# Two attention stages of a two-layer kernel: layer 0 in steps of all four heads, layer 1 with on-chip copies at its start and 0/1 matmuls at its end

## The reference

```python
# layer 0: 16 heads of 64, 4 key/value heads, 2 batches, causal, S = 1024
scores = einsum('bhqd,bhkd->bhqk', q, k) * scale + causal
out = einsum('bhqk,bhkd->bhqd', softmax(scores), v)
return out.reshape(B, S, 1024) @ Wo.T
# layer 1: 16 heads of 8, 4 key/value heads, rope and rmsnorm on q and k, causal
scores = einsum('bthd,bshd->bhts', q, k) / sqrt(8)
out = einsum('bhts,bshd->bthd', softmax(where(causal, scores, -inf)), v)
```

## Time and profile before

| | us |
|---|---|
| median of 3 executions (1544.16 to 1556.04) | 1551.67 |
| the profiled execution | 1549.17 |
| its span, first to last instruction | 1547.5 |
| PE busy (share of the span) | 1316.2 (85%) |
| DVE busy | 1002.8 (65%) |
| ACT busy | 678.9 (44%) |
| POOL busy | 157.7 (10%) |

### The profile page before, as it was taken

One profiled execution on the slowest core, in us unless ns is written; L12 is line 12 of the kernel. 1 busy time (PEld: TensorE's weight loads), 2 busy tenths in 40 slices (PEclk: granted clock), 3 DMA queues, 4 the chain that ended last, 5 costly groups with the idle time before them and its releaser, 6 DMA issues. The chain is left out here.

```text
span 1547.5 us, 19708 instructions
## 1 busy us (share of the span) xinstructions
PE 1316.2 (85%) x6224; PEld 806.3 (52%) x6224; DVE 1002.8 (65%) x1782; ACT 678.9 (44%) x1254; POOL 157.7 (10%) x357
## 2 busy tenths in 40 slices
PE   4789999999999999748999987415898988489997
PEld 3345555555555555435888865313343443156886
DVE  4646566564747472157999985746777875057998
ACT  2133434343333433233666655421466666225664
POOL 0001111111111111100000000211011111010000
PEclk9689999999999999966999997855899999568999
DMA  3110202021111201004777720043122221102220
GB/s 98 28 32 5 57 5 60 11 54 34 30 37 27 50 14 32 15 21 92 157 148 146 160 60 1 1 138 80 27 49 60 50 47 29 53 21 77 76 102 28
DMA packets 42400, 85.59 MB, mean 55 GB/s; under 512 B 13392, under 2 KB 31480, under 8 KB 37368
## 3 DMA queue, kind: packets, MB, share of 16 engines
q1 hardware_dynamic: 42336, 84.78, 23.1%
HBM read 67.38 MB, written 8.45 MB: 49 GB/s over the span
## 5 line engine op out<-in xcount | busy, mean ns | idle before, releaser
L652 ACT ACTIVATE shared<-ps 128x1024 f32<-128x1024 f32 (+7 forms) x256 | 165.8, 650 | 359.8 <-PE ps L501 359.2
L516 PE MATMUL ps<-shared,Vg 128*65 128x512 f32 (+3 forms) x768 | 291.0, 487 | 11.3 <-POOL shared L683 8.5
L1227 PE MATMUL ps<-qA 128*128 128x512 f32 x960 | 254.3, 402 | 10.1 <-POOL qA L1337 10.1
L567 DVE TENSOR_REDUCE mraw<-ps 128x1 f32<-128x512 f32 (+3 forms) x304 | 195.9, 659 | 90.0 <-PE ps L468 62.1
L969 DVE TENSOR_REDUCE mraw<-ps 128x2 f32<-128x1024 f32 (+3 forms) x160 | 173.9, 1114 | 77.5 <-PE ps L889 59.5
L1227 PEld LDWEIGHTS ps<-qA 128*128 128x128 f32 x960 | 183.1, 194 | 60.6 <-POOL qA L1337 11.8
L1013 ACT ACTIVATE shared<-ps 128x512 f32<-128x512 f32 (+2 forms) x320 | 154.4, 564 | 127.8 <-PE ps L905 127.5
L499 PE MATMUL ps<-qA,kH 128*128 128x512 f32 (+3 forms) x384 | 168.2, 446 | 2.7 <-DMA qB<-mT 2.7
L462 PE MATMUL ps<-kH,qA 128*128 128x512 f32 (+3 forms) x384 | 163.5, 466 | 6.0 <-DVE qA L560 2.8
L516 PEld LDWEIGHTS ps<-shared,Vg 128*65 128x65 f32 x768 | 98.4, 138 | 118.7 <-issue 83.7
L1239 PE MATMUL ps<-qA,kH 128*128 128x512 f32 x480 | 136.1, 392 | 4.1 <-DVE qA L1353 4.0
(11 more groups left out here) (229 smaller groups left out, 1561.4 us busy)
## 6 DMA issues: line engine op xcount, KB each, us to landing
shared<-comb SPq DMA_DIRECT2D x92, 256.0 KB, 4.3
qB<-qA SPq DMA_DIRECT2D x8, 1024.0 KB, 7.1
rB<-a0rec_dram SPq DMA_DIRECT2D x8, 1024.0 KB, 7.4
shared<-comb SPq DMA_DIRECT2D x7, 1024.0 KB, 4.4
q_split<-qA SPq DMA_DIRECT2D x8, 512.0 KB
qA<-q_split SPq DMA_DIRECT2D x16, 256.0 KB, 4.4
rB<-a1rec_dram SPq DMA_DIRECT2D x32, 128.0 KB, 2.7
e0wUp<-in_w SPq DMA_DIRECT2D x48, 64.0 KB, 4.6
```

Source lines behind the costliest of these rows:

```text
L516: ins = nc.tensor.matmul(O[0:65, lo:hi], k.Vg[par][:, kt, :], k.PT[:, slot % PTR, lo:hi], start=(kt == 0), stop=(kt == 4 * ch + 3))
L567: ins = nc.vector.tensor_reduce(out, bank[:, 0:n_h * width].rearrange("p (h w) -> p h w", w=width), AX, ALU.max)
L652: nc.scalar.activation(k.PT[:, slot % PTR, kt * P:S], score_banks(slot)[:, kt * P:S], ACT.Exp, scale=scale).then_inc(p_full, 1)
L1227: ins = nc.tensor.matmul(bank[0:M, :], w[par][:, at:at + M], h[:, cols], start=(r == 0), stop=(r == 2))
```

## The change

**Layer 0's attention** takes the form that layer 1's already has: 12 units (qc, kt) per group with all four heads, written out without a loop. Scores go to three banks of 512 columns. The values of a unit are 12 matmuls with 32 stationary columns: v is cut into two halves of 32 columns, two heads with two halves each fill the four column quarters (bank 5 for heads 0 and 1, bank 6 for 2 and 3), and four further matmuls with ones give the sums of the four heads, 32 times each, in bank 7. `Vg` and its copies are gone. Values come two steps behind the scores (LAG), P has three buffers (RING). Jobs are laid behind the score matmuls of a step only. O and sums are copied out twice per group, by ACT (one bank) and DVE (two). Group 0 starts scores of its first query half when that half is prepared, the second half's jobs are laid into steps 0 to 3; the last turn of a group ("turn" of its second half) runs in the first step of the group itself. For the last half of the last group, DVE takes the reciprocal of the sums in PSUM, two matmuls with a 0/1 matrix (`sel64`) bring them to the heads' rows, and DVE multiplies.

**Layer 1.** q and k of groups 0 and 1 are copied from SBUF to SBUF: 32 DMAs on SP and 32 on ACT's own queue, of 8 rows x 1024 columns each. For the other groups q is stored once rather than twice, in the next stage, by 12 DMAs that ACT issues ahead of its first exp; the load reads it twice. POOL clears group 2's buffers, which overlap `qh`, when these stores have landed. The last group's outputs go through two pairs of 0/1 matmuls (`pick`), a reciprocal of 512 columns and a product, straight into `oT`.

```diff
+    UNITS = [(0, kt) for kt in range(4)] + [(1, kt) for kt in range(TPB)]
+    NU = len(UNITS)
+    STEPS = NU * G
+    RING = 3
+    LAG = 2
+    SCORE_BANKS = 3
+    U = 1 + REP // 2
+
...
+        size = max(1, 512 // (512 - unit_lo(n)) // 2 * 2) if 512 - unit_lo(n) <= 256 else 1
+        return [tuple(range(h, h + size)) for h in range(0, REP, size)]
...
+    def woven(g):
+
+        some = [("max", g, 0, j) for j in range(len(MAXES[0]))]
+        more = [("max", g, 1, j) for j in range(len(MAXES[1]))]
+        out = [("proj", g, 0, u) for u in range(U)] + [("proj", g, 1, 0)]
+        out += some[0:3] + [("proj", g, 1, 1)] + some[3:6] + [("proj", g, 1, 2)] + some[6:]
+        return out + more[0:3] + [("turn", g, 0, 0)] + more[3:]
+
...
+    plan = {-1: jobs_of(0, 0)}
+    spread_over(jobs_of(0, 1), 0, 4)
+    spread_over(woven(1), 4, NU)
+    for g in range(2, G):
+        spread_over([("turn", g - 1, 1, 0)] + woven(g), NU * (g - 1), NU * g)
+    plan.setdefault(NU * (G - 1), []).insert(0, ("turn", G - 1, 1, 0))
+    for g in range(G):
+        plan.setdefault(NU * g + 10, []).append(("fin", g, 0, 0))
+        plan.setdefault(NU * (g + 1) + 6, []).append(("fin", g, 1, 0))
...
+        size = -(-len(fills) // len(heads))
+        return [(hs, fills[size * i:size * (i + 1)]) for i, hs in enumerate(heads)]
...
-        O = k.ps[:, 6 * 512:8 * 512]
...
+        O = [k.bank(5), k.bank(6)]
+        SUMS = k.bank(7)
...
+                def values(n):
...
+                        pe.wait_ge(o_act, 2 * g + qc)
+                        pe.wait_ge(o_dve, 2 * g + qc)
+                    lo = unit_lo(n)
+                    first, last = kt == 0, closes(n)
+                    for p in range(2):
+                        for i in range(2):
+                            for half in range(2):
+                                at = 2 * i + half
+                                v = k.V[:, b * TPB + kt, kv * hd + half * CT:kv * hd + (half + 1) * CT]
+                                nc.tensor.matmul(O[p][CT * at:CT * (at + 1), lo:512], v,
+                                                 probs(n)[:, 2 * p + i, lo:512], start=first, stop=last,
+                                                 skip_group_check=True)
+                    for h in range(REP):
+                        ins = nc.tensor.matmul(SUMS[CT * h:CT * (h + 1), lo:512], k.ones[:, 0:CT],
+                                               probs(n)[:, h, lo:512], start=first, stop=last, skip_group_check=True)
+                    ins.then_inc(pv_done, 1)
+
+                for idx in due[-1]:
+                    job(idx)
+                for n in range(STEPS + LAG):
+                    for at, (hs, fills) in enumerate(parts(n)):
+                        if hs:
+                            scores(n, first_score[n] + at, hs)
+                        for idx in fills:
+                            job(idx)
+                    if n >= LAG:
+                        values(n - LAG)
+                pe.wait_ge(o_dve, 2 * G)
+                for p in range(2):
+                    nc.tensor.matmul(score_bank(p), k.sel64[:, p, :], k.S64[:, :], start=True,
+                                     stop=True).then_inc(spread_full, 1)
+                job(index["fin", G - 1, 1, 0])
+
+            @block.vector
+            def _(dve):
...
+                def copy_out(n):
...
+                    nc.vector.tensor_copy(k.S64[:, :], SUMS)
+                    nc.vector.tensor_copy(k.oU64[:, 1, cols], O[1]).then_inc(o_dve, 1)
...
+                for n in range(STEPS + LAG):
+                    if n > LAG and closes(n - LAG - 1):
+                        copy_out(n - LAG - 1)
+                    at = n % NU
+                    if at in (3, 5) and n >= NU:
+                        (recips if at == 3 else normalise)(n // NU - 1, 1)
+                    if at in (7, 9):
+                        (recips if at == 7 else normalise)(n // NU, 0)
+                    for idx in due.get(n, []):
+                        take(idx)
+                cols = slice(512, 1024)
+                dve.wait_ge(pv_done, STEPS)
+                nc.vector.reciprocal(k.S64[:, :], SUMS).then_inc(o_dve, 1)
+                for p in range(2):
+                    dve.wait_ge(spread_full, p + 1)
+                    if p == 0:
+                        dve.wait_ge(o_act, 2 * G)
+                        dve.wait_ge(on_done, 2 * G - 2)
+                    ins = nc.vector.tensor_tensor(k.oN64[:, p, cols], k.oU64[:, p, cols], score_bank(p), ALU.mult)
...
+                nc.scalar.copy(k.oU64[:, 0, 512:1024], O[0])
+                nc.scalar.copy(k.oU64[:, 1, 512:1024], O[1]).then_inc(o_act, 1)
...
+                def pick(qc):
+
+                    pe.wait_ge(o_copied, 2 * (G - 1) + qc + 1)
+                    pe.wait_ge(x_free, NJ * G)
+                    for what in range(2):
+                        ins = nc.tensor.matmul(k.bank(3 + 2 * qc + what)[LAST, :], k.sel8[:, what, :],
+                                               oU[(G - 1) % 2][:, qc * 512:(qc + 1) * 512], start=True, stop=True)
+                    ins.then_inc(x_full, 1)
...
+                    if n == STEPS - 5:
+                        pick(0)
+                pick(1)
...
+                    nc.vector.reciprocal(k.rB[LAST, cols], k.bank(3 + 2 * qc)[LAST, :]).then_inc(rec_done, 1)
+                    dve.wait_ge(rec_done, G + qc)
+                    nc.vector.tensor_tensor(oT[LAST, S + qc * 512:S + (qc + 1) * 512], k.rB[LAST, cols],
+                                            k.bank(4 + 2 * qc)[LAST, :], ALU.mult)
...
+                for b in range(B):
+                    act.wait_ge(in_ld[b], landed(b))
+                for b in range(B):
+                    for part in range(2):
+                        cols = slice(part * T + b * S, part * T + (b + 1) * S)
+                        act.dma_start(q_dram[:, part * hd:(part + 1) * hd, b * S:(b + 1) * S],
+                                      qh[:, cols].bitcast(F32)).then_inc(stored, 16)
+                        for copy in range(2):
+                            at = (2 * part + copy) * hd
+                            act.dma_start(k_dram[:, at:at + hd, b * S:(b + 1) * S],
+                                          kh[:, cols].bitcast(F32)).then_inc(stored, 16)
...
+                pool.wait_ge(stored, 16 * STORES)
...
-                load(0)
-                load(1)
-                sp.wait_ge(cleared, 1)
-                load(2)
...
+                sp.wait_ge(stored, 16 * STORES)
+                load(2)
...
-                gather_sums(G - 1)
-                spread(G - 1)
-                store(G - 1)
-                sp.wait_ge(o_st, 16 * REP * G)
-                sp.dma_start(oT[:, S:T], o_dram[:, :, S:T].rearrange("h d q -> (h d) q")).then_inc(oT_ld, 16)
+                sp.dma_start(oT[0:LAST.start, S:T], o_dram[0:NH - REP, :, S:T].rearrange("h d q -> (h d) q"))\
+                    .then_inc(oT_ld, 16)
...
+                act.wait_ge(padded, 2)
+                for b in range(B):
+                    act.wait_ge(low, 2 * CPB * (b + 1))
+                    for part in range(2):
+                        src = kh[0:hd, part * T + b * S:part * T + (b + 1) * S].bitcast(F32)
+                        for copy in range(2):
+                            for i in range(2):
+                                at = 64 * i + (2 * part + copy) * hd
+                                act.dma_start(kZero[b][at:at + hd, :].bitcast(F32), src).then_inc(k.a1_in[b], 16)
+                                act.dma_start(kOne[b][at:at + hd, :].bitcast(F32), src).then_inc(k.a1_in[b], 16)
...
+                    for i in range(2):
+                        for j in range(2):
+                            head = (i + 2 * j) * hd
+                            for part in range(2):
+                                src = qh[head:head + hd, part * T + b * S:part * T + (b + 1) * S].bitcast(F32)
+                                for copy in range(2):
+                                    at = 64 * i + (2 * copy + part) * hd
+                                    sp.dma_start(Q[b][at:at + hd, j, :].bitcast(F32), src).then_inc(k.a1_in[b], 16)
```

731 lines of the change are left out of this document (371 added, 360 removed).

## The result

The changed kernel takes 1536.7 us in the median against 1547.1 for the kernel before, each run 20 times: a ratio of 0.9934, with a 95% interval of 0.9913 to 0.9956. That is 10 us of the 47 forecast. The profiled execution took 1542.7 us (span 1540.9), 6.6 us of span less than that of before.

The account below looks back on a forecast made before the run. PE was taken to set the pace of layer 0's groups at 72.6 us each. The terms -6 -4 -5 -13 -10 -9 sum to -47 us against the profiled 1549.2: 1502 us, range 1472 to 1542.

Parts of the forecast that it names:

- Layer 0, values: Layer 0's value matmuls: three sets of column quarters replace four heads' blocks, -4.5 us a group (-3.0 to -6.3).
- the rival of the halves: Value matmuls: two halves sharing one head's P run one after the other, 15.4 us a group more, 1625; chance 0.05.
- Layer 0, waits: Layer 0's jobs, now only between score matmuls, make PE wait: +3.5 us a group, bounds 0 and +9.5.
- The new waits: Layer 0: 5 us from units with many jobs plus 2 from DVE's copies and products: 7 us a group.
- The hand walk: Layer 0 unit with six maxima, followed: PE waits about 1.0 us, in some five of twelve units.
- The waits of before: Layer 0 in the kernel before: 3.5 us of waits a group, taken from 8.4 us beyond pure column time.
- DVE's order sets the pace: Rival, layer 0: DVE's fixed places hold all jobs, +9.5 us a group instead of +3.5, 1544; chance 0.20.
- Layer 0, head: Layer 0's start: first scores at 62 us, group 1 at 158 against 162, -4 us (-20 to +12).
- Last group and layer 0's tail: End of layer 0: last group without jobs -5 us; tail from values to y without DMAs -13 us.
- Layer 1, head: Before layer 1's attention: copies at 0.55 us each, stores delaying some 2 us, -10 us (0 to -18).
- Layer 1, tail: After layer 1's attention: matmuls, reciprocal and product replace three DMA round trips, 9 us, a gain of -9 (-7 to -11).
- the marks that were to show it: Trace signs, both layers: unit values 2.8 to 3.0 us, period 70 to 73, layer 1's first matmul 17 to 20, others.

Follow-up runs that it names:

- run 20: Not a label, only words of "each run 20 times": changed kernel and kernel before, 20 executions each, medians 1536.7 and 1547.1 us, ratio 0.9934.
- layer 1 alone: The change in layer 1 only, with layer 0 as in the kernel before; measured 0.9929 (0.9896 to 0.9962) of the kernel before.

## Why the prediction was wrong

- **Layer 0, values: direction right, size low.** Forecast -4.5 us a group (-3.0 to -6.3), measured -6.0. The quarters of one head's halves go side by side, so the rival of the halves is out. (The eight records of a block in the earlier trace rows do not start together but in two sets of four, 0.45 us apart; four at a time is all that the argument needs.)
- **Layer 0, waits: this step failed.** Forecast +3.5 us a group, bounds 0 and +9.5; a period of 74.2 with 6.0 us less of values makes it +7.6. The +3.5 were 7 us of new waits less 3.5 us of waits that the kernel before was to have had.
  - *The new waits.* The hand walk took a unit of six maxima and let it stand for all. It left out what the upper bound had named, a projection whose bank is held through ACT's rounding and DVE's subtraction. Two of them stand between maxima in the fifth unit; moving them took 1.8 us a group, and with it the fall of the clock, which the sum had put at full throughout, 1.0. The other 4.8 of the 7.6 are the turnaround of two banks, for which the sum had 7 - 3.5: a third bank took 3.5 us, short reductions 5.1.
  - *The waits of before.* By the rows of waits PE's jobs waited 0.5 us a group for DVE before (the values 1.1 for POOL), not 3.5. With moved projections and short reductions, where little is left to wait for, a group takes 66.3 us, only 0.3 less than 72.6 - 6.0; so the 72.6 can hardly have had 3.5 us of such waits. That is worked out and not shown: no run has the kernel before with short reductions.

  The rival "DVE's order sets the pace" (+9.5) was nearer than the forecast, though the runs name two banks and not the order: a copy taken off DVE gave 0.2, the place of the maxima 0.5, a third bank with DVE's order as it was 3.9. The Trainium skill (TensorEngine Tiling (Array Packing), PSUM Bottleneck) warns that tiling speeds up TensorE and not the emptying of PSUM; the runs agree, with 3.5 to 6.0 us a group, though the banks that held PE were those of the jobs, which are not tiled. Counting DVE's copies, as the prediction did, was no answer to it: fewer of them were left, but the job banks came due faster.
- **Layer 0, head: wrong for the same reason, and by a wrong start.** First scores at 60.2 for the 62 forecast, but 103.4 us from there to group 1 for 96. Three banks make it 89.6. The 162 that the forecast took for the start of group 1 is the end of a stretch in the earlier trace rows; the trace of before has it at 157.5, so its own 158 was no gain. (Its 12.0 us of scores in steps 4 to 11 are 11.1 at its price: 3328 columns x 4 heads x 2 x 0.417 ns.)
- **Last group and layer 0's tail: right.** -5.7 and -13.4 for -5 and -13, 10.6 us from values to y in a range of 9 to 12.
- **Layer 1, head: mechanism right, two sizes off.** A copy costs 0.81 to 0.84 us and not 0.55 (inside the bounds of 0.32 to 1.65), 9 us over 32 of them; the stores delay the rows by 4.0 us and not 2. That is the 10 us. With the stores later and half of the copies out of the way first scores come 15 us sooner than in the change and first exps 12.
- **Layer 1, tail: right.** -11.7 for -9.
- **What the forecast did not hold:** +5.1 us in layer 1's steady part (277.0 for 271.9) and +3.5 behind. From layer 1's first scores to its last values, in the change and in the run of layer 1 alone, which has the same layer 1:

```profile
1059.60:1336.60 277.00, 244.62 (x1899) 105.89 (x1899) 188.56 (x200) 161.44 (x336) 46.16 (x67) 0.88 0.23 46
1059.40:1325.30 265.90, 231.59 (x1899) 101.97 (x1899) 188.00 (x200) 160.73 (x336) 46.19 (x67) 0.94 0.24 48
```

  The same instructions take 11 us more where the mean granted clock is 0.88 and not 0.94. In the other traces with this layer 1 the stretch takes 270.0 to 278.2 us, and what is behind it 194.2 to 197.5; layer 1 as before took 271.9 (clock 0.90) and, behind the changed layer 0, 283.9 (0.83), and 193.8 and 197.0 behind it. So both differences lie within what executions of the same code differ by; what sets the clock is open.

Of the marks that were to show it, first scores, the tail and PE's idle time before maxima came; the values of a unit came a little below theirs (2.72 us for 2.8 to 3.0); period (70 to 73) and first maximum (17 to 20 us after the first copy) did not.

## What to carry to other kernels

When matmuls get shorter, count again what hangs on PSUM: list for each bank how long a job holds it, from its matmul to the last read, with every engine in that chain, and compare with the distance of the jobs. A job with two engines behind it goes where a long block of matmuls without jobs follows. One bank more gave back 3.5 to 3.9 us here of the 6.0 that the shorter matmuls were worth. Before a wait is taken off as one that was there already, look for it in the trace. Many small DMAs cost issue time on their queue; issue first those that the next step needs.

## What was not expected of the hardware

- A copy of 32 KB from SBUF to SBUF takes 0.81 to 0.84 us of its queue when two queues issue at once, 0.76 (SyncE, 12.12 us) and 0.87 (ScalarE) when each issues 16, 0.63 to 0.73 on ScalarE's queue behind them.
- A job between quarter-tiled sets costs about 0.35 us beside its own time: 0.14 us more in the set and some 0.2 more in the job itself (0.45 us for 0.22).
- The clock fell behind 1.9 us of idle in four groups of five, and in none of the same five with that idle and short reductions.
- A reciprocal of 512 columns takes 3.36 us on 128 partitions and on 32 alike.
